# A fused attention and mixture-of-experts kernel: key stores and stack loads issued ahead of weight loads, and the first routing spread anew

## The chip, the cores and the metric
The kernel runs on one core of one Trainium2 chip. The metric is the device time of one launch in microseconds. TensorE (PE), VectorE (DVE), ScalarE (ACT) and GpSimd (POOL) compute, SyncE (SP) issues nearly all DMAs.

## The reference
Input x is 32 batches of 128 rows by 128; ctx has the same shape.

```python
x = x + tanh(g_xattn) * xattn(layernorm(x), ctx, ...)   # 16 heads of 8, keys of x and of ctx
#   q, k, v = layernorm(x) @ Wqkv + b ; qa, ka, va = ctx @ Wqkv_aux + b_aux
#   out = softmax(q k') v * (1 - gate) + softmax(q ka') va * gate ; out @ Wo + bo
x = x + tanh(g_ffn) * ffn(layernorm(x), ...)            # 64 experts of width 64, plus a shared one
#   scores = sigmoid(x @ gate_w.T); best 4 of 8 groups, best 8 experts in them, weights summed to 2.5
#   y = sum over experts e of cw[:, e] * (silu(x @ We_gate[e]) * (x @ We_up[e])) @ We_down[e]
```

## The kernel before
**Two phases.** First the attention over 32 blocks (one batch each), two blocks to a chunk, 16 chunks (NC = 16), four blocks to a body, 8 bodies (LOOPS = 8). Then the experts over 8 pieces of 512 rows, 33 pairs of experts each. The program is written out by hand: each engine has its own order of instructions, and semaphores tie them together.

**A chunk of the attention.** Queries and keys are split into three bf16 parts (`split`, on VectorE for chunks 0 and 1, on GpSimd from chunk 2 on; semaphore `lo_ok` counts its last steps, one for the queries and two for the keys). SyncE stores the parts to DRAM (`store_q` L411, `store_k` L418) and loads them back in another layout, heads one above the other, as `stack_q` (`load_stack_q` L431) and `stack_k` (`load_stack_k` L444). A load waits until its store has landed, and until TensorE has used the chunk three before in the same of three slots (`st_mm`). `clear_shift` (L436) copies zeros from `zero_d` into four rows of the slot. TensorE scores block b + 2 (`round_of_scores`, L1283), VectorE takes the maxima (L991), whose negatives go as rows into `stack_q` by a DMA that ScalarE issues (`shift_rows`, `stack_q<-nmaxT`). Then TensorE scores block b once more, shifted (L1307), ScalarE takes the exponentials (L791), TensorE weighs the values (`weighted`, L1322; it waits for the residual of the block before last), and VectorE adds the residual (L1034).

**SyncE's order in a chunk n** is that of `body` in `on_sp`: load x of n + 4, stack load of q of n + 2, clearing, two loads of expert weights (480 KB in most chunks), store of k of n + 2, stack load of k of n + 2, store of x2 of n - 1, store of q of n + 3. The expert weights are asked for by ScalarE (`high_of`) from chunk 2 on, two pairs a chunk.

**The first routing.** The last body (chunks 14 and 15, blocks k = 0 to 3 of `body` with `last`) also routes the first piece of the experts on VectorE: `first_route`, 14 parts, placed by `ROUTE_AT` at (block k, half-round u). In blocks 0 and 1 VectorE still takes maxima, in 2 and 3 not. TensorE turns the routing weights (`first_turn_w`), ScalarE copies them (`first_wT`, `fwt_ev`), SyncE stores them (L570) and loads them back, broadcast, as combine weights `cwb` (L578, two groups of two loads of 384 KB), which GpSimd's first products (`hidden`, L1631) wait for.

**The start.** SyncE stores zeros from `x2[0]` to `zero_d` (L513) ahead of the first q store.

Of the kernel before, what the change touches and what calls it, by code (L numbers as in the profile page):

```python
# [18 lines left out]
BF16 = mybir.dt.bfloat16  # L19
# [23 lines left out]
E, F = 64, 64  # L43
# [128 lines left out]
def attention(nc, sem, m, m_cw, psum, v):  # L172
    wide = v["wide"]
    x, ctx, x2d, q_d, k_d = v["x"], v["ctx"], v["x2d"], v["q_d"], v["k_d"]
    q0_d, k0_d, zero_d = v["q0_d"], v["k0_d"], v["zero_d"]
# [3 lines left out]
    NEX, NP, gwT, wts_d, cw_in, cwb, GP = (v[n] for n in ("NEX", "NP", "gwT", "wts_d", "cw_in", "cwb", "GP"))  # L179
# [11 lines left out]
    x2 = [m(f"x2_{i}", [P, CH, P], F32) for i in range(2)]  # L191
# [92 lines left out]
    def part(name, n):  # L284
# [33 lines left out]
    zeros_ok, zeros_st = sem("zeros_ready"), sem("zeros_stored")  # L318
# [32 lines left out]
                + [(n, c, r) for n in range(LIGHT, NC - 1) for c in range(CH) for r in (0, 3)]  # L351
                + [(NC - 1, 0, 1), (NC - 1, 0, 2), (NC - 1, 1, 0)])
    assert len(SPLIT_AT) == NP
    ROUTE_AT = {(0, 5): (0,), (0, 7): (1, 2), (1, 1): (3,), (1, 3): (4,), (1, 5): (5,), (1, 7): (6, 7), (2, 1): (8, 9),
                (2, 3): (10, 11), (2, 5): (12, 13)}

    STATS_AT = ((0, 5), (0, 7), (1, 1))

# [40 lines left out]
    def on_sp(sp):  # L399
# [7 lines left out]
        def store_q(n, i):  # L407

            wait(sp, lo_ok, SPLITS * n + 1)
            dst = q_d[n].rearrange("s p c t -> p s (c t)")  # L410
            sp.dma_start(dst[:, 0:PART], parts_q[i][:]).then_inc(q_st[i], 16)  # L411
            sp.dma_start(dst[:, PART], parts_q[i][:, Q_AT[0]]).then_inc(q_st[i], 16)

        def store_k(n, i):

            wait(sp, lo_ok, SPLITS * (n + 1))
            dst = k_d[n].rearrange("s p c a t -> p s (c a t)")
            sp.dma_start(dst[:, 2:2 + PART], parts_k[i][:]).then_inc(k_st[i], 16)  # L418
            sp.dma_start(dst[:, 0:2], parts_k[i][:, 0:2]).then_inc(k_st[i], 16)
# [14 lines left out]
        def clear_shift(n):  # L434

            sp.dma_start(stack_q[n % NST][64:68].rearrange("p h c t -> p (h c t)"), zero_d).then_inc(shift_zero[n % NST], 16)  # L436

        def load_stack_k(n):

            s = n % NST  # L440
            wait(sp, st_mm, UNITS * CH * (n - NST + 1))
            wait(sp, k_st[n % 2], 32 * ((n + 1) // 2))
            for half in (1, 0):
                sp.dma_start(stack_k[s][PARTS_AT[half]:PARTS_AT[half] + ROWS_S].rearrange("p h c a t -> p (h c a t)"),  # L444
                             pairs(k_v[n], 2 * DH, half, 2 * HH * TC)).then_inc(stk[half][s], 16)
# [53 lines left out]
        def store_x2(n, i):  # L499
# [9 lines left out]
        sp.dma_start(bo_row[:], one(v["bo"]).to_broadcast([P, P])).then_inc(wo_in, 16)  # L509
        load_x(2)  # L510
        load_x(3)
        sp.wait_ge(zeros_ok, 1)
        sp.dma_start(zero_d.rearrange("r (j t) -> (r j) t", j=4), x2[0][0:16].rearrange("p c t -> p (c t)").bitcast(BF16)  # L513
                     ).then_inc(zeros_st, 16)
        store_first_q()
        store_first_k(0)
        sp.wait_ge(stack_zero, 2)
# [6 lines left out]
        load_stack_q(1)  # L524
        load_stack_k(1)
        store_q(2, 0)

        def body(g, last):
            for j in range(2):
                n, i = 2 * g + j, j  # L530
                if n == 0:
                    sp.wait_ge(w_zero, 3)
                if n + 4 < NC:
                    load_x(n + 4)
                if not last:
                    if n == 0:
                        sp.wait_ge(stack_clear, NST)
                    load_stack_q(n + 2)
                    if n == 1:
                        sp.wait_ge(zeros_st, 16)  # L540
                    if n + 2 >= NST:
                        clear_shift(n + 2)
                if g < LOOPS - 2:
                    expert_weights(g, j)
                elif not last and j == 0:
                    expert_weights(g, 0)
                    expert_weights(g, 1)
                if not last:
                    store_k(n + 2, i)
                    load_stack_k(n + 2)  # L550
                if n > 0:
                    store_x2(n - 1, 1 - j)
                if n + 3 < NC:
                    store_q(n + 3, 1 - i)
                if g == 0:
                    small_weights(j)
                if g == LOOPS - 3 and j == 1:

                    for t in range(2):
                        sp.wait_ge(x2_st[t], 16)  # L560
                    sp.dma_start(xld[:], x2_four[0]).then_inc(xl_in, 16)
# [11 lines left out]
        for i in range(2):  # L573
            sp.wait_ge(q_st[i], 32 * (NC // 2 - 1 + i))
            sp.wait_ge(k_st[i], 32 * (NC // 2 - 1 + i))
        for gr in range(2):
            for half in range(2):
                sp.dma_start(cwb[gr][half * F:(half + 1) * F, :, :],  # L578
                             wts_v[0][half][GP * gr:GP * (gr + 1)].unsqueeze(0).to_broadcast([F, GP, T])
                             ).then_inc(cw_in[gr], 16)  # L580
# [145 lines left out]
    def on_act(act):  # L726
# [134 lines left out]
        def body(g, left):  # L861
            last, before_last = left == 0, left == 1
            for k in range(BODY):
                b, n, i, odd = BODY * g + k, 2 * g + k // CH, k // CH, k % CH
                first = b == 0
                more = not (last and i == 1)
                for r in range(ROUNDS):
                    exps(b, r)
                    if r == 0 and not first:
                        copy_o(b - 1, 1 - odd)  # L870
                    if r == 0 and not odd and n > 0 and n + 3 < NC:
                        norm(n + 3)
                    if (n, odd, r) in SPLIT_AT:
                        q = SPLIT_AT.index((n, odd, r))
                        if 2 * q + 1 < E - LAST_E:
                            act.wait_ge(w_in[0], 16 * 4 * (1 + max(0, -((FIRST_E - 2 * q - 2) // EACH_E))))
                        if q == NP - 1:
                            act.wait_ge(w_zero, 3)
                            act.wait_ge(w_in[1], 16 * 3)
                        if q == (E - LAST_E) // 2:  # L880
                            act.wait_ge(w_in[2], 16 * 4)
                        high_of(q)
                    if r == 1 and not (last and k == BODY - 1):
                        shift_rows(b + 1)
                    if before_last and k == 2 and r < 2:
                        if r == 0:
                            act.wait_ge(k_st[0], 32 * (NC // 2 - 1))
                        first_norm(r)
                    if before_last and k == 3 and r == 1:
                        first_operand()  # L890
                        act.wait_ge(lo_ok, SPLITS * NC)
                        first_xT()
                    if last and k == 0 and r == 0:
                        first_exp()
                    if first and r == 1:
                        norm(3)
                    if (odd, r) == ((0, 2) if last else (0, 1)) and more:
                        if first:
                            act.wait_ge(v_zero, 6)
                        copy_v(n + 1, (i + 1) % 2)  # L900
                    if odd and r == 1 and n + 3 < NC:
                        copy_qk(n + 3)
                    if r == 2 and not first:
                        copy_att(b - 1, 1 - odd)
                    if not odd and r == 2 and n + 3 < NC:
                        evac_t(n + 3, 1 - i)
                    if before_last and k == 2 and r == 3:
                        first_gate()
                    if last and k == 3 and r == 1:
                        first_wT()  # L910

        for g in range(LOOPS - 2):
# [8 lines left out]
    def on_dve(dve):  # L921
# [135 lines left out]
        def first_route(part):  # L1057
# [3 lines left out]
            sig, sp = f_sig_p, f_sc_p  # L1061
            halves = lambda t: t.rearrange("p k (g h e) -> p k g h e", g=NG, h=2)
            if part == 0:
                dve.wait_ge(fe_ok, 1)
                nc.vector.tensor_scalar(sig, f_sig[:].rearrange("p k e -> p (k e)"), 1.0, None, ALU.add).then_inc(fs_ok, 1)
                dve.wait_ge(fs_ok, 1)
                nc.vector.reciprocal(sig, sig).then_inc(fs_ok, 1)
            if part == 1:
                dve.wait_ge(fs_ok, 2)
                logit = sig.rearrange("p (k g h e) -> p k g h e", k=K, g=NG, h=2)  # L1070
                bias = gbias[:].unsqueeze(1).to_broadcast([P, K, E]).rearrange("p k (g h e) -> p k g h e", g=NG, h=2)
                for h, to in ((0, sp), (1, f_sc_s[:])):
                    tt(to.rearrange("p (k g) e -> p k g e", k=K), logit[:, :, :, h], bias[:, :, :, h],
                       ALU.add).then_inc(frt, 1)
# [161 lines left out]
    def on_pe(pe):  # L1236
# [171 lines left out]
        def body(g, left):  # L1408
            last, before_last = left == 0, left == 1
            for k in range(BODY):  # L1410
# [4 lines left out]
                for r in range(ROUNDS):  # L1415
# [41 lines left out]
                        first_turn_x()  # L1457
                    if before_last and k == 3 and r == 3:
                        first_logits()
                    if last and k == 3 and r == 0:  # L1460
                        first_turn_w()

        for g in range(LOOPS - 2):
# [558 lines left out]
```

## Time and profile before

| | us |
|---|---|
| median of 3 runs | 912.15 (909.82 to 915.29) |
| the profiled execution | 910.34 |
| its span | 908.5 |
| busy: TensorE, VectorE, GpSimd, ScalarE | 850.6, 677.4, 617.1, 563.5 |
| mean granted clock of TensorE | 0.983 |
| attention | 0 to about 329.6 |
| experts | about 329.6 to the end |

All times are counted from the start of the span. In a timeline row the first number is the start, the second the duration, and the bracket gives how long the engine was idle before and what ended that. SPq is SyncE's queue: a row there is the issue of a DMA, not its transfer.

### The profile page before, as it was taken

To read this page: it belongs to the slowest core of one execution; us is meant where nothing else is said; L and a number is where in the kernel's file an instruction comes from. 1 tells how busy PE (TensorE), PEld (TensorE's weight loads), DVE (VectorE), ACT (ScalarE), POOL (GpSimd) and SP (SyncE) were. 2 spreads that over 40 slices of the span, in tenths; PEclk is the share of its full clock that TensorE was granted. 3 is DMA by queue.
4 is the path that set the end of the run, shared out by engine and by line. 5 is a ranking of instruction groups with operands and counts; after the bars stand their busy time and mean duration, and the time that the engine had idled before them with its cause. 6 is when DMAs were issued, how large, how long until landed. Compare 5 with 4: busy or idle time off the path is not lost.

```text
span 908.5 us, 20053 instructions
## 1 busy us (share of the span) xinstructions
PE 850.6 (94%) x6765; PEld 647.7 (71%) x6765; DVE 677.4 (75%) x1653; ACT 563.5 (62%) x963; POOL 617.1 (68%) x579
## 2 busy tenths in 40 slices
PE   5789889899998889999999999999999999999997
PEld 3356556566665567888888888887888888888885
DVE  6788769686887857967866976977777776786665
ACT  4277668686777667557557556555656655755554
POOL 2455675576655337887877877787777777878785
PEclk9999999898999999999999999999999999999999
DMA  5666667666765044654654654754654655465552
GB/s 134 181 159 160 174 158 180 157 173 160 171 166 142 10 101 116 151 138 112 164 122 121 158 141 109 162 124 112 165 129 123 152 127 141 108 159 123 138 140 62
DMA packets 113755, 125.46 MB, mean 138 GB/s; under 512 B 28005, under 2 KB 76021, under 8 KB 112217
## 3 DMA queue, kind: packets, MB, share of 16 engines
q1 hardware_dynamic: 110776, 123.66, 55.6%
q10 hardware_dynamic: 2880, 0.59, 0.4%
q8 instruction: 49, 0.80, 0.4%
q14 instruction: 50, 0.40, 0.2%
HBM read 103.73 MB, written 19.97 MB: 136 GB/s over the span
## 4 chain that ended last, share of the span: by engine, by line
PE 70%; DMA 14%; POOL 4%; SPq 4%; DVE 3%; issue 3%; ACT 1%; POOLq 0%; ACTq 0%; DVEq 0%
PE bank L1928 18%; PE bank L1930 18%; PE bank L1929 18%; DMA stack_k<-k_scratch 6%; PE bank L1322 3%; DMA k_scratch<-parts_k 3%; PE bank L1307 2%; PE bank L1261 2%; DMA stack_q<-nmaxT 2%; PE bank L1283 2%; DMA q_scratch<-parts_q 1%; POOL hid L1631 1%; PE bank L1249 1%; SPq L431 1%; PE bank L1905 1%
## 5 line engine op out<-in xcount | busy, mean ns | idle before, releaser
L1631 POOL TENSOR_TENSOR hid<-act,cwb 128x512 f32<-128x512 f32 x264 | 430.7, 1639 | 134.3 <-DVE act L1846 92.2
L1680 ACT ACTIVATE silu<-bank 128x512 f32<-128x512 f32 x264 | 157.3, 596 | 209.6 <-PE bank L1930 209.5
L1846 DVE TENSOR_TENSOR act<-silu,bank 128x512 f32<-128x512 f32 x264 | 180.4, 684 | 142.8 <-ACT silu L1680 136.4
L1928 PE MATMUL bank<-xhi,weights_hi 128*128 128x512 f32 x528 | 210.0, 398 | 0.0
L1930 PE MATMUL bank<-xlo,weights_hi 128*128 128x512 f32 x528 | 207.8, 394 | 0.0
L1929 PE MATMUL bank<-xhi,weights_lo 128*128 128x512 f32 x528 | 207.3, 393 | 0.0
L1850 DVE TENSOR_TENSOR hlo<-hid,hhi 128x512 fp32r<-128x512 f32 x264 | 200.8, 761 | 2.7 <-ACT hhi L1685 2.5
L991 DVE TENSOR_REDUCE mx<-bank 128x4 f32<-128x512 f32 x256 | 164.7, 686 | 43.3 <-PE bank L1283 40.0
L1685 ACT ACTIVATE hhi<-hid 128x512 fp32r<-128x512 f32 x264 | 165.0, 625 | 8.0 <-POOL hid L1631 7.5
L791 ACT ACTIVATE prob<-bank 128x1024 f32<-128x1024 f32 x128 | 131.0, 1024 | 60.9 <-PE bank L1307 59.1
L1930 PEld LDWEIGHTS bank<-xlo,weights_hi 128*128 128x128 f32 x528 | 99.2, 188 | 22.3
L1928 PEld LDWEIGHTS bank<-xhi,weights_hi 128*128 128x128 f32 x528 | 99.3, 188 | 21.4 <-ACT silu L1680 0.3
L1929 PEld LDWEIGHTS bank<-xhi,weights_lo 128*128 128x128 f32 x528 | 99.4, 188 | 20.8
L1928 PE MATMUL bank<-hhi,weights_hi 128*128 128x512 f32 x264 | 104.4, 395 | 2.8 <-DVE hlo L1850 2.7
L1929 PE MATMUL bank<-hhi,weights_lo 128*128 128x512 f32 x264 | 103.6, 392 | 0.0
L1930 PE MATMUL bank<-hlo,weights_hi 128*128 128x512 f32 x264 | 103.3, 391 | 0.0
L1283 PE MATMUL bank<-stack_k,stack_q 48*128 48x256 bf16 (+1 forms) x512 | 60.3, 290 | 28.0 <-DMA stack_k<-k_scratch 21.6
L1322 PE MATMUL bank<-prob,V 128*32 128x128 f32 x2048 | 84.2, 283 | 0.0
L1322 PEld LDWEIGHTS bank<-prob,V 128*32 128x32 f32 x2048 | 48.9, 110 | 21.9 <-issue 15.5
L1928 PEld LDWEIGHTS bank<-hhi,weights_hi 128*128 128x128 f32 x264 | 49.6, 188 | 15.7 <-issue 2.4
L1930 PEld LDWEIGHTS bank<-hlo,weights_hi 128*128 128x128 f32 x264 | 49.7, 188 | 11.4
L1929 PEld LDWEIGHTS bank<-hhi,weights_lo 128*128 128x128 f32 x264 | 49.7, 188 | 11.2
(227 smaller groups left out, 939.9 us busy)
## 6 DMA issues: line engine op xcount, KB each, us to landing
cwb<-wts_scratch SPq DMA_DIRECT2D x176, 384.0 KB, 5.4
stack_k<-k_scratch SPq DMA_DIRECT2D x30, 384.0 KB
k_scratch<-parts_k SPq DMA_DIRECT2D x15, 384.0 KB, 4.5
stack_q<-q_scratch SPq DMA_DIRECT2D x30, 192.0 KB
k_scratch<-parts_k SPq DMA_DIRECT2D x15, 256.0 KB, 4.9
q_scratch<-parts_q SPq DMA_DIRECT2D x15, 192.0 KB, 3.0
xin<-in_x_dram SPq DMA_DIRECT2D x16, 128.0 KB, 2.8
cin<-in_ctx_dram SPq DMA_DIRECT2D x16, 128.0 KB, 3.3
```

The lines of the kernel that those rows point to most:

```text
L791: act.activation(prob[pair % RP][:].rearrange("p u k -> p (u k)"), wide[:], ACT.Exp, scale=scale).then_inc(p_ok, 1)
L991: nc.vector.tensor_reduce(mx[par][:, 2 * f:2 * f + 2, 2 * r:2 * r + 2].rearrange("p a h -> p h a"), s_bank[f].rearrange("p (h a k) -> p h ...
L1283: ins = nc.tensor.matmul(s_bank[f][:, e * TC:(e + 1) * TC], q_of(n)[at, 2 * r + e, c, :], k_of(n)[at, 2 * r + e, c].rearrange("p a t -> p ...
L1322: ins = nc.tensor.matmul(to, V[i][:, a, par, h, :], prob[(ROUNDS * b + u // 2) % RP][:, j % 2, (2 * a + j // 2) * P:(2 * a + j // 2 + 1) * P],
L1631: pool.tensor_tensor(h_buf[k][:], a_buf[k][:], cwb[slot][:, q % GP, :], ALU.mult).then_inc(h_ok, 1)
L1680: act.activation(s_buf[k % RS][:], g_bank[k % 2][:], ACT.Silu).then_inc(s_ok, 1)
L1685: act.activation(hhi[k % RH][:], h_buf[k % RS][:], ACT.Copy).then_inc(hh_ok, 1)
L1846: nc.vector.tensor_tensor(a_buf[k % RS][:], s_buf[k % RS][:], u_bank[k % 3][:], ALU.mult).then_inc(a_ok, 1)
L1850: nc.vector.tensor_tensor(hlo[k % RH][:], h_buf[k % RS][:], hhi[k % RH][:].bitcast(F32), ALU.subtract).then_inc(hl_ok, 1)
L1928: nc.tensor.matmul(bank, w[0], mh, start=first, stop=False)
L1929: nc.tensor.matmul(bank, w[1], mh, start=False, stop=False)
L1930: return nc.tensor.matmul(bank, w[0], ml, start=False, stop=last)
```

## The change
In each chunk SyncE issues the key store and the stack load of the keys ahead of the two weight loads. The store of zeros moves from ahead of the first q store to behind the stack loads of chunk 1 and the q store of chunk 2. The second group of the first combine weights is issued only when the first has landed. The reciprocal of the first sigmoids is cut in four steps of 64 columns, and the parts of the first routing get other places; their transposes on TensorE and the copy on ScalarE move one round later.

```diff
-    ROUTE_AT = {(0, 5): (0,), (0, 7): (1, 2), (1, 1): (3,), (1, 3): (4,), (1, 5): (5,), (1, 7): (6, 7), (2, 1): (8, 9),
-                (2, 3): (10, 11), (2, 5): (12, 13)}
+    ROUTE_AT = {(0, 3): (0,), (0, 5): (1 / 4,), (0, 7): (2 / 4,), (1, 3): (3 / 4,), (1, 5): (1,), (1, 7): (2,), (2, 1): (3, 4),
+                (2, 3): (5, 6, 7), (2, 5): (8, 9, 10), (2, 6): (11, 12, 13)}
...
         load_x(3)
-        sp.wait_ge(zeros_ok, 1)
-        sp.dma_start(zero_d.rearrange("r (j t) -> (r j) t", j=4), x2[0][0:16].rearrange("p c t -> p (c t)").bitcast(BF16)
-                     ).then_inc(zeros_st, 16)
         store_first_q()
...
         store_q(2, 0)
+        sp.wait_ge(zeros_ok, 1)
+        sp.dma_start(zero_d.rearrange("r (j t) -> (r j) t", j=4), x2[0][0:16].rearrange("p c t -> p (c t)").bitcast(BF16)
+                     ).then_inc(zeros_st, 16)
...
                         clear_shift(n + 2)
+                    store_k(n + 2, i)
+                    load_stack_k(n + 2)
                 if g < LOOPS - 2:
                     expert_weights(g, j)
                 elif not last and j == 0:
                     expert_weights(g, 0)
                     expert_weights(g, 1)
-                if not last:
-                    store_k(n + 2, i)
-                    load_stack_k(n + 2)
...
         for gr in range(2):
+            if gr == 1:
+                sp.wait_ge(cw_in[0], 32)
...
-                    if last and k == 3 and r == 1:
+                    if last and k == 3 and r == 2:
                         first_wT()
...
+            if 0 < part < 1:
                 dve.wait_ge(fs_ok, 1)
-                nc.vector.reciprocal(sig, sig).then_inc(fs_ok, 1)
+                cols = slice(int(4 * part - 1) * E, int(4 * part) * E)
+                nc.vector.reciprocal(sig[:, cols], sig[:, cols]).then_inc(fs_ok, 1)
             if part == 1:
-                dve.wait_ge(fs_ok, 2)
+                dve.wait_ge(fs_ok, 4)
+                nc.vector.reciprocal(sig[:, 3 * E:], sig[:, 3 * E:]).then_inc(fs_ok, 1)
+                dve.wait_ge(fs_ok, 5)
...
-                    if last and k == 3 and r == 0:
+                    if last and k == 3 and r == 1:
                         first_turn_w()
```

## Rows read from the trace of the kernel before
**Rows 1.** Windows: stretch, its length, busy time of each engine, clock, DMA share, GB/s.
```profile
58.84:296.50 237.66, 213.55 (x3427) 146.06 (x3427) 185.65 (x457) 172.70 (x274) 143.78 (x234) 0.95 0.67 165
132.90:136.30 3.40, 3.40 (x30) 2.54 (x23) 1.15 (x4) 1.85 (x4) 2.43 (x3) 0.51 0.42 110
296.50:329.60 33.10, 28.73 (x488) 18.07 (x487) 24.49 (x89) 24.06 (x36) 9.01 (x11) 0.95 0.09 23
345.00:908.50 563.50, 555.26 (x2474) 450.93 (x2473) 416.41 (x967) 333.06 (x595) 432.38 (x272) 1.00 0.54 131
```
**Rows 2.** Waits of TensorE, 58.5 to 296.5: us in total, times, longest.
```profile
PE bank L1283 <- DMA stack_k<-k_scratch: 20.9, 9, 4.0
```
**Rows 3.** Timeline of TensorE, 112 to 150 us, rows behind a wait.
```profile
112.19 0.40 PE L1307 MATMUL bank<-stack_q,stack_k 64*128 64x128 bf16 x8 [0.86 <-DMA stack_q<-nmaxT]
132.05 0.47 PE L1283 MATMUL bank<-stack_k,stack_q 48*128 48x256 bf16 x4 [3.97 <-DMA stack_k<-k_scratch]
149.40 0.40 PE L1307 MATMUL bank<-stack_q,stack_k 64*128 64x128 bf16 x8 [0.50 <-DMA stack_q<-nmaxT]
```
**Rows 4.** Timeline of SyncE's queue, parts of three chunks.
```profile
116.64 0.60 SPq L418 DMA_DIRECT2D k_scratch<-parts_k  x1
...
124.47 1.56 SPq L444 DMA_DIRECT2D stack_k<-k_scratch  x2
...
127.67 0.93 SPq L412 DMA_DIRECT2D q_scratch<-parts_q  x1
...
132.90 1.56 SPq L431 DMA_DIRECT2D stack_q<-q_scratch  x2
...
135.45 0.73 SPq L488 DMA_DIRECT2D weights_raw<-in_L_ffn_We_down_dram  x1
136.22 0.60 SPq L418 DMA_DIRECT2D k_scratch<-parts_k  x1
...
141.94 1.56 SPq L444 DMA_DIRECT2D stack_k<-k_scratch  x2
...
283.54 0.58 SPq L418 DMA_DIRECT2D k_scratch<-parts_k  x1
...
288.00 2.47 SPq L444 DMA_DIRECT2D stack_k<-k_scratch  x2
```
**Rows 5.** Timeline of GpSimd: last steps of a q split and a k split.
```profile
126.57 0.67 POOL L634 TENSOR_TENSOR parts_q<-rest,parts_q 128x256 bf16<-128x256 f32 x1
...
132.08 0.67 POOL L634 TENSOR_TENSOR parts_k<-rest,parts_k 128x256 bf16<-128x256 f32 x1
```
**Rows 6.** Chain of work that ended last: start, duration, two rows of maxima.
```profile
143.77 5.58 DMA stack_q<-nmaxT
...
216.60 6.79 DMA stack_q<-nmaxT
```
**Rows 7.** List of DMA issues: count, size, median us from issue to landing.
```profile
weights_raw<-in_L_ffn_We_gate_dram SPq DMA_DIRECT2D x5, 320.0 KB, 5.1
```
**Rows 8.** Timeline of VectorE at the start: last step of the first q split.
```profile
12.93 0.42 DVE L1166 TENSOR_TENSOR parts_q<-rest,parts_q 128x256 bf16<-128x256 f32 x1
```
**Rows 9.** Timeline of VectorE in the last body: parts of the first routing.
```profile
303.26 1.75 DVE L1067 RECIPROCAL f_sigmoid<-f_sigmoid 128x256 f32<-128x256 f32 x1
...
309.27 0.21 DVE L1083 TENSOR_TENSOR f_mid_b<-f_top_p,f_top_s 128x64 f32<-128x64 f32 x1
...
316.71 0.15 DVE L1108 MATCH_REPLACE8 f_grest<-f_gtop,f_gs 128x8 f32<-128x8 f32 x1
...
322.46 0.43 DVE L1149 TENSOR_TENSOR f_rep<-f_masked,f_wsum_p 128x256 f32<-128x256 f32 x1
```
**Rows 10.** Timeline of TensorE, 308 to 340 us, two rows behind a wait.
```profile
308.18 0.22 PE L1347 MATMUL bank<-ident_bf,nmax 128*128 128x128 bf16 x1 [1.01 <-DVE nmax L1003]
...
339.95 0.47 PE L1928 MATMUL bank<-hhi,weights_hi 128*128 128x512 f32 x1 [2.01 <-DVE hlo L1850]
```
**Rows 11.** Chain of work that ended last, at the start of the experts.
```profile
329.21 7.40 DMA cwb<-wts_scratch
```

## The prediction
> **What bounds the kernel now.** I read the windows first, to split the span into stages. From 345 us to the end (the experts) TensorE is busy 555.3 of 563.5 us at full clock [rows 1]; nothing of the change lies there, so that stage is taken as it is. The attention's steady part, 58.84 to 296.50, is another matter: TensorE is busy 213.6 of 237.7 us and its mean clock is 0.95 [rows 1]. Its list of waits says for whom: 20.9 us in nine waits are for stack_k [rows 2].
>
> TensorE's own timeline shows how a chunk (two batch rows, 13 of them in this stretch, so 18.28 us each) goes. It restarts at 112.19 and is back at the next chunk's scores at 132.05 - 3.97 = 128.08: 15.9 us of work. Then it waits 3.97 us for stack_k; the next chunk runs 132.05 to 148.90, 16.85 us, and waits 0.50 us for the row of maxima [rows 3]. That chunk took 1.0 us longer because the granted clock was half (0.51) from 132.9 to 136.3, right behind the wait [rows 1]. A mean clock of 0.95 is 237.7 x 0.05 / 0.5 = 24 us at half clock, seven such stretches; at 1.0 to 1.3 us each they cost some 8 us. So per chunk: 15.9 work, 1.85 waiting (24.1 / 13), 0.6 slow clock.
>
> SyncE's timeline shows why stack_k is late. Its slot comes free only when the chunk before has used it, so the load must fit into one chunk, behind the key store. One round [rows 4]: k store issued at 116.64, k load at 124.47 (7.8 us: SyncE stood on the store's landing), landed at 132.0, 7.5 us later. The q store, whose last part was ready at 127.24 [rows 5] and which was issued at once, landed only at 132.87, 0.9 us behind the k load; only then did the q load of the next chunk go out (132.90), then the weights (135.02 to 136.18), then the k store at 136.22, though GpSimd had the last k part at 132.75 [rows 5]; k load 141.94. So the stage turns in a loop: q landed, q load and row clearing 2.1 us, weights' issue 1.2, k store to k load 5.7 to 7.8, k load 7.3, q store behind it 0.9: 17.3 to 19.3 us, which spans the 18.28 seen.
>
> **Part 1: key store and stack load ahead of the weights.** Three things change.
> (a) Issue: the store leaves before the two weight issues, 1.2 us here, but never before GpSimd is ready. Over the chunks of this stretch SyncE's weight issues took 1.1 to 2.6 us and in two of them GpSimd was the later; I take 1.1.
> (b) The store no longer shares the DMA engines with 480 KB of weights. The one store that had none ahead of it went from 283.54 to 288.00, 4.46 us, against 5.72 (136.22 to 141.94) and 7.83 in the round above [rows 4]; I take 4.3 for 5.9, a gain of 1.5. Bounds: nothing, and 3.3.
> (c) The weights now stand behind the stack load, on the same queue, and ahead of the x2 store and of the q store of the next chunk. Everything on SyncE's queue behind them is later. The k load itself should keep its 7.3 us.
> Now the loop anew, from TensorE's restart T. GpSimd's q parts are ready at T + 15.05 and its k parts at T + 20.56 (127.24 and 132.75 less 112.19) [rows 3, 5]; they hang on VectorE's and TensorE's place in the chunk, not on the DMAs. Three bounds follow for the chunk length C.
> First, the k path, over two chunks: 20.56 + 0.3 + 4.3 + 7.3 = 32.4, so C = 16.2.
> Second, the q path: q landed to k store 2.1, k load 4.3, landed 7.3, weights X, q store 0.9: C = 14.6 + X. X has no row, as weights never stood there. Below: 0, if they fill gaps of the load (the DMA share was 0.67 [rows 1]). Above: 5.1 us, the whole median landing of a weight transfer [rows 7]. 480 KB at this stage's mean of 165 GB/s [rows 1] is 2.9; partly overlapped I take X = 2.1, C = 16.7.
> Third, the row of maxima: issued at T + 11.7 in the chunk with the slow clock, T + 10.4 without it, landed 5.58 to 6.79 us later beside a k load [rows 6]: C = 16.0 to 17.2. This is what is late next when stack_k is not.
> All lie above the work of 15.9. I take C = 16.7: waits of 0.8 us a chunk. After waits of 0.50 us no slow stretch is seen, after 3.97 one is [rows 1, 3], so the slow clock should mostly go with them. The gain is 13 x (18.28 - 16.7) = 20.5 us; with C = 15.9 it is 31, with 17.6 it is 9. The weights themselves come some 6 us later, landing near the start of the next chunk; ScalarE first asks for a chunk's weights half a chunk after that, so it stays covered; without that cover its exponentials would stand behind the wait.
> A rule speaks against this edit. The Trainium skill, DMA: Bandwidth & Descriptors, section "Queues, rings and completion order", says that each DMA engine takes the descriptors of one ring in ring order, and that SyncE has one ring per engine; by it the weights pass whole ahead of the q store. The trace agrees in one place: the q store, issued three microseconds into the k load, landed 0.9 us behind it. By that rule X is nearer to the weights' full time than to nothing, which is the rival below.
>
> **Part 2: zeros stored later.** The first q store waits for a part that VectorE had only at 12.93 + 0.42 = 13.35 [rows 8], and SyncE issued it 0.1 us later. So the zero store's own issue (0.5 us) was hidden behind that wait; 0.1 us at most is gained. At its new place it is followed by the wait of chunk 0, and its readers come 20 us later: nothing.
>
> **Part 3: sigmoids in four, route later.** In the last body (chunks 14 and 15) nothing is transferred and VectorE sets the pace: the stage 296.50 to 329.60 has TensorE busy 28.7 of 33.1 us and its clock is 0.95 [rows 1]. The reciprocal of 256 columns stands 1.75 us in front of the maxima [rows 9]; TensorE waited 1.01 us for VectorE at 308.18 [rows 10], and in this stretch 4.2 us in eight waits. Four steps of 1.75 / 4 = 0.44 us, one between two maxima, fit where VectorE has slack. Parts 3 to 7 of the route (23 instructions from 309.27 to 316.86, 2.6 us with their steps) [rows 9] move into the block where no maxima are left, so the routing weights are done 2.6 us later against that block's start: 322.9 becomes 325.5 in the old time, less what the two blocks before gain. The residual stands behind it on VectorE, and the last block's weighted sums wait for that; 0.5 us is lost there. Gained in blocks one and two: about 2.5 us of waits and 1.0 us of slow clock. Net 3.0, bounds 1 and 4.5.
>
> **Part 4: combine weights in two steps.** Their transposes and their copy move one round (1.6 us) nearer to the end of the attention. The store of 2.0 us and the loads follow: before, four loads shared the engines and the first pair landed at 336.61, 7.40 us after its second issue [rows 11]. Alone, that pair of 384 KB each should take what a stack load of the same size takes from its second issue, 6.7 us or a little less; I take 6.0, so 1.4 of the 1.6 comes back. TensorE waited 2.01 us for what hangs on it [rows 10]; I leave that. The second pair goes out 6 us later, needed three hidden products (4.2 us) and a root later: just in time, with TensorE two pairs ahead. SyncE's wait also holds the last x2 store and the third group's loads by some 1.5 us; both have that slack. Net 0, bounds -2 and +2.
> The fit of the Trainium skill (DMA: Bandwidth & Descriptors, section "Anatomy of one DMA"), a fixed 2.0 us and then 436 GB/s, would land that pair in 3.8 us; the sum would then be 2 us lower. No row here moves 768 KB that fast.
>
> **Sum.** 20.5 + 0.1 + 3.0 + 0 = 23.6 us. The profiled execution took 910.34 us for a span of 908.5, 1.8 less than the median of 912.15. 912.15 - 23.6 = 888.5; I say 889.
>
> **The rivals.**
> Everything vanishes (C = 15.9, X near 0, the row of maxima keeps pace): 31 + 3 + 2 = 36 us, 877. For it: the share of 0.67 leaves room. Against it: the row of maxima was late by itself in four chunks where stack_k was not, as at 149.40 [rows 3].
> The weights take the gap partly back: X = 3 to 3.5, C = 17.6 to 18.1, waits long enough that some of the slow stretches stay: 5 to 9 us here and 3 in the last body, 903 down to 900. For it: the order on the queue.
> Slower: the loop is closed by the weights. Where 14.6 + X passes 18.28, that is from X = 3.7 us on, this edit loses. With X = 5.1 a chunk is 19.7, 13 of them lose 18 us, less 3 from the last body: 927; just past the point, at X = 4.2, 912 + 7 - 3 = 916. Against it: in the old order the same weights lengthened the k store by only 1.5 us.
> It doesn't do what it says: if GpSimd's k parts were always the later, (a) is nothing, and (b) alone is left; that is in my range (C = 17.3).
>
> **Chances.** Forecast (C from 16.2 to 17.3, 880 to 897) 0.60; all vanishes (below 880) 0.11; partly taken back (897 to 907) 0.18; about no change 0.05; slower 0.06. The range 879 to 903 leaves out about 2 in 10. Within 0.5% (4.6 us, about what a measurement can tell from no change) are 907.6 to 916.7. Faster 0.88, same 0.06, slower 0.06.
>
> **What would show it.** Right: k store to k load 4 to 4.6 us; stack_k waits down from 20.9 to under 8 us in all; mean clock of the steady part 0.98 or more; waits for the row of maxima up; the q store landing 2 to 3 us after TensorE's restart. Wrong: a q load issued more than 3.5 us after the restart (X too small), a k load of over 8 us (weights interleaved), chunks still of 18 us, or TensorE's wait before the first down projection over 3 us.

## The result

The changed kernel takes 913.38 us (median of 20 runs) beside 909.87 us for the kernel before (20 runs); the ratio is 1.0037, 95% interval 1.002 to 1.0055. Where 889 us was forecast, it is 3.5 us slower. (The forecast took its 23.6 us off 912.15 us, a median of 3 runs; with 20 runs the kernel before is at 909.87.) The profiled execution has a span of 912.1 us and a mean clock of 0.963.

The attention's steady part, windows of the kernel after over 58.8 to 298.3 (its last chunk starts 1.5 us later than before), columns as in [rows 1], and TensorE's waits in it beside [rows 2]:

```profile
58.80:298.30 239.50, 216.85 (x3436) 148.28 (x3436) 185.90 (x457) 173.19 (x275) 144.54 (x236) 0.94 0.69 164
```
```profile
PE bank L1312 <- DMA stack_q<-nmaxT: 11.8, 8, 2.5
PE bank L1288 <- DMA stack_k<-k_scratch: 11.6, 6, 3.6
```

The chunk is as long as it was, 239.5 / 13 = 18.4 us. The wait for stack_k fell from 20.9 to 11.6 us, and the wait for the row of maxima took its place: 11.8 us in eight places, where the kernel before has 3.9 us in five. The clock is not better either: 0.94.

SyncE's queue in one round of the kernel after, which answers to [rows 4]:

```profile
134.59 1.56 SPq L431 DMA_DIRECT2D stack_q<-q_scratch  x2
...
137.05 0.38 SPq L418 DMA_DIRECT2D k_scratch<-parts_k  x1
...
142.62 1.56 SPq L444 DMA_DIRECT2D stack_k<-k_scratch  x2
144.23 0.59 SPq L485 DMA_DIRECT2D weights_raw<-in_L_ffn_We_up_dram  x1
...
147.92 0.39 SPq L411 DMA_DIRECT2D q_scratch<-parts_q  x1
148.35 1.21 SPq L412 DMA_DIRECT2D q_scratch<-parts_q  x1
...
153.98 1.56 SPq L431 DMA_DIRECT2D stack_q<-q_scratch  x2
...
164.80 2.75 SPq L411 DMA_DIRECT2D q_scratch<-parts_q  x1
```

TensorE at the two restarts around it, beside [rows 3], and the chain of work for one row of maxima, beside [rows 6]:

```profile
131.43 0.47 PE L1288 MATMUL bank<-stack_k,stack_q 48*128 48x256 bf16 x4 [1.93 <-DMA stack_k<-k_scratch]
149.86 0.47 PE L1288 MATMUL bank<-stack_k,stack_q 48*128 48x256 bf16 x4 [1.14 <-DMA stack_k<-k_scratch]
```
```profile
218.62 7.35 DMA stack_q<-nmaxT
```

The stack load goes out at 142.62 and has landed when TensorE restarts at 149.86; the q store, issued in full by 149.56 with the weights in front, lets the q load go only at 153.98, 4.1 us behind TensorE's restart, where before it was 0.9 us behind. Even its issue now takes 1.21 us, and 2.75 us a chunk later, where [rows 4] has 0.93.

The loop in three legs, each the mean over 12 chunks from SyncE's timeline (q load issue to k store issue; to the stack load's issue; to the next q load's issue). "Row" is the mean time from the issue of a row of maxima to TensorE's restart, over the rows that TensorE waited for (1 in e9, 5 to 11 in the other runs). These are the late rows of each run, not its average row:

| kernel | q load to k store | to k load | to next q load | sum | row |
|---|---|---|---|---|---|
| before | 3.8 | 6.0 | 8.7 | 18.5 | 5.9 |
| after | 2.4 | 4.6 | 11.5 | 18.5 | 6.6 |
| the order alone (e1) | 2.2 | 4.7 | 11.3 | 18.2 | 6.7 |
| no weights in these chunks (e4) | 2.7 | 4.4 | 9.2 | 16.3 | 6.0 |
| weights between (e6) | 2.8 | 4.6 | 9.7 | 17.1 | 5.8 |
| weights behind the q store (e7) | 2.3 | 5.1 | 9.7 | 17.2 | 5.9 |
| new order, whole rows (e8) | 2.4 | 4.6 | 10.8 | 17.8 | 6.7 |
| old order, whole rows (e9) | 3.5 | 5.3 | 8.9 | 17.7 | 6.0 |
| the change, weights between (f2) | 2.6 | 4.8 | 9.3 | 16.7 | 5.7 |

The first two legs gained 2.8 us and the third gave 2.8 back.

In the last body, TensorE and VectorE of the kernel after (beside [rows 9, 10]):

```profile
307.63 0.22 PE L1352 MATMUL bank<-ident_bf,nmax 128*128 128x128 bf16 x1 [0.26 <-DVE nmax L1004]
...
316.90 0.22 PE L1352 MATMUL bank<-ident_bf,nmax 128*128 128x128 bf16 x1 [1.66 <-DVE nmax L1004]
...
326.48 1.03 PE L1327 MATMUL bank<-prob,V 128*32 128x128 f32 x16 [1.83 <-issue]
...
342.92 0.47 PE L1933 MATMUL bank<-hhi,weights_hi 128*128 128x512 f32 x1 [2.19 <-DVE hlo L1855]
```
```profile
325.69 0.42 DVE L1154 TENSOR_TENSOR f_rep<-f_masked,f_wsum_p 128x256 f32<-128x256 f32 x1
326.04 0.34 DVE L1035 SCALAR_TENSOR_TENSOR x<-bank,tg_x,xin 128x128 f32<-128x128 f32 x1
```

The wait at the first row of maxima fell from 1.01 to 0.26 us, but a wait of 1.83 us is new; it ends at 326.48, when VectorE has done the residual (326.04 + 0.34). The profile calls it "issue": it names nothing that ended it. That it was the residual is shown by f3 below.

### The profile page after: what moved, and what is told of

The parts are those of the page before. It is cut to its first block, busy times and chain, and to the rows that moved or that the text cites. A ratio compares the mean times of both kernels' runs of the same rounds, so it can differ in the third digit from the quotient of the medians.

```text
span 912.1 us, 20056 instructions
## 1 busy us (share of the span) xinstructions
PE 852.4 (93%) x6765; PEld 649.2 (71%) x6765; DVE 681.1 (75%) x1656; ACT 563.3 (62%) x963; POOL 616.0 (68%) x579
## 4 chain that ended last, share of the span: by engine, by line
PE 73%; DMA 14%; DVE 3%; issue 3%; POOL 2%; SPq 2%; ACT 2%; ACTq 0%; POOLq 0%; DVEq 0%
PE bank L1933 18%; PE bank L1935 18%; PE bank L1934 18%; DMA stack_k<-k_scratch 5%; DMA stack_q<-nmaxT 5%; PE bank L1327 4%; PE bank L1312 3%; PE bank L1266 2%; PE bank L1288 2%; PE bank L1254 1%; PE bank L1334 1%; DMA cwb<-wts_scratch 1%; DMA k_scratch<-parts_k 1%; POOL hid L1636 1%; PE bank L1910 1%
## 5 line engine op out<-in xcount | busy, mean ns | idle before, releaser
L1288 PE MATMUL bank<-stack_k,stack_q 48*128 48x256 bf16 (+1 forms) x512 | 60.0, 289 | 17.7 <-DMA stack_k<-k_scratch 12.7
L1312 PE MATMUL bank<-stack_q,stack_k 64*128 64x128 bf16 (+1 forms) x1024 | 53.4, 226 | 13.4 <-DMA stack_q<-nmaxT 11.9
L1312 PEld LDWEIGHTS bank<-stack_q,stack_k 64*128 64x128 bf16 (+1 forms) x1024 | 30.3, 97 | 41.0 <-issue 19.7
```

The costliest lines, as they stand in the source:

```text
L1312: ins = nc.tensor.matmul(st_bank[f][:, (2 * a + e) * P:(2 * a + e + 1) * P], k_of(n)[at, at_half, c, a, :], q_of(n)[at, at_half, c, :], st ...
```

## The experiments

Theory A: the weights have to pass somewhere in the loop; behind the stack load they hold up the q store and the row of maxima, by as much as they had held up the key store. Rivals: the order does gain, and other parts of the change eat it; or something else, such as GpSimd's splits, holds the loop whatever the weights do.

### The parts alone

**e1_order**: the kernel before with the new order of SyncE only.

```diff
+                    store_k(n + 2, i)
+                    load_stack_k(n + 2)
                 if g < LOOPS - 2:
                     expert_weights(g, j)
...
-                if not last:
-                    store_k(n + 2, i)
-                    load_stack_k(n + 2)
```

> The new order of SyncE alone, on the kernel before. Theory A (the weights, now between the k load and the q store, close the loop again): the whole stays within 3 us of the kernel before, chunks of 18 to 18.6 us, k store to k load near 4.7 us, the q load issued 3 us or more after TensorE's restart. Rival (the order gains what was forecast and another part eats it): 12 to 20 us faster, chunks of 16.7 to 17.3 us.

Measured: ratio to the kernel before 1.0012 (0.999 to 1.0034). So the forecast's 20 us are not there in the order alone; that rival is out. Its chunks take 18.2 us, as theory A says. Its waits of TensorE, 58.2 to 294.3:

```profile
PE bank L1306 <- DMA stack_q<-nmaxT: 12.8, 8, 2.8
PE bank L1282 <- DMA stack_k<-k_scratch: 11.8, 5, 3.3
```

**e2_route**: the sigmoids in four, the new `ROUTE_AT`, the turn and the copy one round later, nothing else.

> Only the sigmoids in four and the new places of the route, with the turn and the copy one round later. Theory: VectorE frees its first two blocks (2 to 3 us fewer waits there), but TensorE waits 1.5 to 2 us in the last block for the residual that stands behind the route, and the weights' copy is later: in all 1 to 2 us slower. Rival, as forecast: 3 us faster.

Measured: 1.0013 (0.9992 to 1.0035), not told from no change. In the trace, from TensorE's wait in the second round of the last body to the first down projection it is 43.3 us (296.49 to 339.79), before 41.9 (298.03 to 339.95): 1.4 us longer, with the same wait of 1.83 us.

**e3_cw**: the combine weights in two steps, nothing else.

```diff
         for gr in range(2):
+            if gr == 1:
+                sp.wait_ge(cw_in[0], 32)
```

> Only the combine weights in two steps. The first pair lands 1.5 us earlier than in the kernel before (6.6 instead of 8.1 us from its first issue). Theory: TensorE's wait before the first down projection, 2.0 us, falls to 0.5 and the slow clock behind it goes: 1.5 to 3 us faster. Rival: the second pair or the third group, issued later, is now waited for: no gain.

Measured: 1.0012 (0.9989 to 1.0036). The wait before the first down projection did fall by 1.0 us:

```profile
342.97 0.47 PE L1930 MATMUL bank<-hhi,weights_hi 128*128 128x512 f32 x1 [1.02 <-DVE hlo L1852]
```

A microsecond is below what the runs can tell. No slow clock followed the wait in this trace (1.00 from 330 to 345, 0.89 before), but ScalarE's normalised x2 was then late for TensorE by 0.9 us at 347.18, so nothing more came of it.

### No weights in the steady chunks

**e4_after_allw**: the kernel after, with all expert weight loads issued in chunk 0.

```diff
-                if g < LOOPS - 2:
-                    expert_weights(g, j)
-                elif not last and j == 0:
-                    expert_weights(g, 0)
-                    expert_weights(g, 1)
+                if n == 0:
+                    for gg in range(LOOPS - 1):
+                        expert_weights(gg, 0)
+                        expert_weights(gg, 1)
```

> The changed kernel with every expert weight load issued in chunk 0, so that the later chunks have no weights on the queue at all. The first two chunks get longer by some 20 us; only the chunks from 4 on are read. Theory A: without weights the loop has 14.6 us of its own, chunks fall to 16.2 to 16.6 us (key path), little slow clock. Rival B (something else than the weights holds the loop, such as GpSimd's splits or the row of maxima): chunks stay at 17.5 us or more.

Measured in one execution (922.55 us, with the load of all weights ahead): TensorE restarts at 125.25 and at 273.00, nine chunks later, 16.4 us each. Its window and waits there:

```profile
125.30:273.00 147.70, 140.50 (x2377) 96.34 (x2378) 128.60 (x318) 119.87 (x189) 104.59 (x173) 1.00 0.58 158
```
```profile
PE bank L1311 <- DMA stack_q<-nmaxT: 3.9, 5, 1.5
PE bank L1287 <- DMA stack_k<-k_scratch: 3.5, 3, 1.5
```

The clock is full and 7.4 us of waits are left in nine chunks. So the weights' 480 KB cost 2 us a chunk, in the old place (18.3 us) as in the new (18.4). GpSimd's splits don't hold the loop at 18 us; that rival is out.

### Where they stand

**e6_between**: the kernel before, weights behind the key store and ahead of SyncE's wait for its landing.

```diff
+                    store_k(n + 2, i)
                 if g < LOOPS - 2:
                     expert_weights(g, j)
...
                 if not last:
-                    store_k(n + 2, i)
                     load_stack_k(n + 2)
```

> Kernel before, with the two weight loads of a chunk issued behind the key store and ahead of SyncE's wait for its landing, so that they fill the pause of the queue before the stack load. Theory A (the weights take DMA time wherever they stand in the loop q load, k store, k load, q store): the k load, behind them, lands later by what the k store gains; chunks of 17.5 to 18.3 us, at most 5 us faster in all. Rival (only the place matters, the pause is free): chunks near 16.8 us, 15 us or more faster.

Measured: 0.984 (0.9809 to 0.987), 894.61 us, 14.8 us faster. One round of its SyncE queue:

```profile
203.13 0.38 SPq L418 DMA_DIRECT2D k_scratch<-parts_k  x1
203.55 0.49 SPq L419 DMA_DIRECT2D k_scratch<-parts_k  x1
204.07 0.64 SPq L485 DMA_DIRECT2D weights_raw<-in_L_ffn_We_up_dram  x1
205.09 1.13 SPq L488 DMA_DIRECT2D weights_raw<-in_L_ffn_We_down_dram  x1
207.61 1.58 SPq L444 DMA_DIRECT2D stack_k<-k_scratch  x2
```

The weights are issued in the 4.5 us in which SyncE waits for the key store anyway, and the stack load goes out as soon as without them (4.6 us behind the key store's issue, 4.4 in e4). They don't move wholly in that pause: they land 4.9 to 5.8 us behind their issue (median), so part of them moves beside the stack load. From 165.99 to 263.98, six chunks, it is 16.3 us a chunk; the six chunks before took 17.8 (59.44 to 165.99), and the mean of the table is 17.1. So most of the weights' 2 us is gone, not all of it, and why the early chunks are slower is open. My theory A in its strict form (they cost the same wherever they stand in the loop) falls here; the place decides.

**e7_behind_q**: the kernel before, k store and k load first, the weights behind the q store.

```diff
-                if g < LOOPS - 2:
-                    expert_weights(g, j)
-                elif not last and j == 0:
-                    expert_weights(g, 0)
-                    expert_weights(g, 1)
-                if not last:
                     store_k(n + 2, i)
                     load_stack_k(n + 2)
...
                     store_q(n + 3, 1 - i)
+                if g < LOOPS - 2:
+                    expert_weights(g, j)
+                elif not last and j == 0:
+                    expert_weights(g, 0)
+                    expert_weights(g, 1)
```

> Kernel before, with k store and k load first and the weight loads behind the q store, last in the chunk. The q store lands soon behind the k load again (2 to 3 us after its issue), but the q load of the next chunk is behind the weights. Theory A: the q load lands later and the k store behind it is stretched, chunks of 17.3 to 18.3 us. Rival (what cost the gain was only the q store's place behind the weights): chunks of 16.8 us, 15 us or more faster.

Measured: 0.9897 (0.9854 to 0.9939), 897.90 us, 11.5 us faster, with chunks of 17.2 us. The third leg fell from 11.3 (e1) to 9.7 us and the row of maxima lands in 5.9; the second leg grew from 4.7 to 5.1, with the weights now issued just ahead of q load and key store. Between the two expectations, nearer to the rival; e6 was 3.3 us faster, but the two intervals overlap.

### Pieces or bytes

The gate and up weights are read in pieces of 256 bytes, the down weights in 512. **e8_flat_new** has the new order and **e9_flat_old** the old one, both with the same bytes read as whole rows of 2560 bytes; the experts then compute with permuted weights.

```diff
-                         up[e0:e0 + ne].rearrange("e d f -> d e f")).then_inc(done, 16)
+                         up[e0:e0 + ne].rearrange("e d f -> (e d f)").rearrange("(p e f) -> p e f", p=P, e=ne)
+                         ).then_inc(done, 16)
...
```

> The new order alone, with the same bytes of expert weights read as whole contiguous rows (2560 and 2560 bytes) instead of pieces of 256 and 512 bytes. The weights stand in a wrong order in SBUF, so the experts compute with permuted weights. If the small pieces are what makes the weights dear: chunks of 16.5 to 17.2 us, 12 to 20 us faster than the kernel before. If it is their bytes: chunks stay at 17.8 us or more, within 5 us.

> The same contiguous weights in SyncE's old order; the experts again compute with permuted weights. If the small pieces are dear: faster than the kernel before by 5 us or more, and slower than the new order with the same weights by some 5 us (there the order would pay). If it is bytes: as the kernel before.

Measured: 0.9939 (0.991 to 0.9968) and 0.9957 (0.9934 to 0.9981), with 95,962 packets in place of 113,755. The pieces are worth 4 to 6 us in either order, so neither expectation holds in full, and the order makes no difference that can be told. As a chunk is still 17.7 to 17.8 us and not 16.4, most of the weights' cost is not in the pieces. e8 shows which wait is then left, 58 to 297:

```profile
PE bank L1308 <- DMA stack_q<-nmaxT: 16.7, 11, 2.3
PE bank L1284 <- DMA stack_k<-k_scratch: 5.1, 2, 3.7
```

With the weights behind the stack load the rows that TensorE waited for still took 6.7 us to land, and they ended its wait in 11 places. In the old order (e9) it did so once, with 0.9 us.

### The whole change with the weights elsewhere, and the route mended

**f2_after_between**: the kernel after, with the weights where e6 has them.

> The whole change, with only the weights put between key store and k load instead of behind the k load. Theory (the place of the weights alone took the gain): 11 to 15 us faster than the kernel before, 14 to 18 faster than the changed kernel; the row of maxima lands in 5.8 us instead of 6.6, the q load goes out 3 us behind the q store instead of 4.7 to 5.4. Rival (the other parts of the change hold the time): under 8 us faster than before.

Measured: 0.9827 (0.9777 to 0.9877), 894.88 us: 16 us faster than the kernel before, and 18.5 less than the change's 913.38. Its chunks are 16.7 us, the rows of maxima that TensorE waited for land in 5.7, and its steady part has a clock of 0.99. The one thing moved is the weights, so in the change it was their place behind the stack load that took the gain. Even so, no run reaches the 23.6 us of the forecast.

**f3_residual_first**: e2 with parts 11 to 13 of the route behind the residual.

```diff
-                (2, 3): (5, 6, 7), (2, 5): (8, 9, 10), (2, 6): (11, 12, 13)}
+                (2, 3): (5, 6, 7), (2, 5): (8, 9, 10), (2, 7): (11, 12, 13)}
```

> The sigmoids and the route as in the change, alone on the kernel before, but parts 11 to 13 of the route behind the residual on VectorE, not ahead of it. Theory (TensorE's 1.83 us wait in the last block is for that residual): the wait goes, and 1.5 to 2.5 us with it against the run with the route alone, so 0 to 1 us faster than the kernel before. Rival (the wait is for the routing weights): it stays, or moves to the turn of the weights.

Measured: 0.9985 (0.9957 to 1.0014). The wait of 1.83 us is gone, so it was for the residual; the stretch from the second round to the first down projection is 42.4 us (296.10 to 338.46), 0.9 less than e2 and 0.4 more than before. Its last body had more slow clock in this trace (0.81 from 312 to 330, against 0.91 in e2 and 0.95 before), so what the later route costs by itself stays open. The runs can't tell either difference.

**f1_between_cw** (e6 with the combine weights in two steps) and **f4_between_cw_route** (f2 with f3's route):

> Weights between key store and k load (the earlier run with this order took 14.8 us off), and the combine weights in two steps. Theory: the two are in different stages and add: TensorE's wait before the first down projection falls by 1 us again, so 15 to 17 us faster than the kernel before. Rival: the combine weights in two steps are worth nothing or cost: 13 to 15 us.

> All together: weights between key store and k load, combine weights in two steps, route with the residual first, zeros later. If everything adds: 16 to 19 us faster than the kernel before and the fastest of all. Rival: the later route still costs, and this is slower than the weights between alone with the two steps.

Measured: 0.9812 (0.977 to 0.9853), 895.10 us, and 0.9807 (0.9757 to 0.9857), 894.62 us. Both, e6 and f2 lie within each other's intervals. All beat both kernels; which of the four is best isn't told. In f1 the wait before the first down projection is 0.77 us (1.93 in e6). In f4 TensorE then waits 0.63 us for the routing weights themselves, at 304.74.

## Why the prediction was wrong

**What was right.** The reading of the loop, and its first two legs: the k store leaves earlier (3.8 to 2.4 us, against 1.1 forecast gain) and lands sooner (6.0 to 4.6, forecast 5.9 to 4.3). Without weights I gave 14.6 us to the q path and 16.2 to the k path; e4 has 16.4.

**Part 1 (c), the q path: the step that failed.** C = 2.1 + 4.3 + 7.3 + X + 0.9 with X = 2.1 was 16.7. e1 measures 2.2, then 4.7, then 11.3 for the rest; the sign that the prediction names for too small an X came too (in the kernel after the q load goes out 4.1 us behind the restart, over 3.5). In the chunks where TensorE waited for stack_k, the load landed 7.8 us behind its issue (7.4 before), which leaves 3.5 for X + 0.9; with the 0.9 kept, X = 2.6. The terms were 0.1 (q load), 0.4 (key store), 0.5 (stack load) and 0.5 (X) too small, all with the same sign: together 1.5 us a chunk, 20 us in 13. That "the k load itself should keep its 7.3 us" was wrong, and X was taken near its lower half on the ground of a DMA share of 0.67, a mean over the chunk. What counts is probably the share behind the stack load, where the x2 store, the q store and the x loads stand too; what that row of transfers shows is that its members land later (in e1; before: 2.9 us for the q store, 5.1 for the weights):

```profile
q_scratch<-parts_q SPq DMA_DIRECT2D x12, 192.0 KB, 4.4
weights_raw<-in_L_ffn_We_gate_dram SPq DMA_DIRECT2D x5, 320.0 KB, 7.6
```

So the 5.1 us from [rows 7], my upper bound for X, was itself a time of the old place. The rule that spoke against the edit pointed the right way, though X stayed below the 3 to 3.5 us of its rival. The Trainium skill (DMA: Bandwidth & Descriptors, section "Queues, rings and completion order") has each engine take one ring's descriptors in order; the trace agrees in direction: e7, which only moves the weights behind the q store, gave 1.6 us of the third leg back.

**Part 1, the row of maxima.** I had its bound as C = 16.0 to 17.2 and took it to stay. For the rows that TensorE waited for it rose with the edit: 5.9 us to land before, 6.7 in e1 and e8, 5.8 to 5.9 in e6 and e7. The row is 16 KB on ScalarE's queue, and I had asked for every wait behind the weights on SyncE's queue only. 10.4 + 6.7 = 17.1, and with a slow clock ahead of it 11.7 + 6.7 = 18.4. How the 18.2 us of e1 divide between the q path and the row I can't say: in e1 the row ended the wait in eight places and stack_k in five; with whole rows (e8) the third leg is 10.8 us and the row ends 11 of 13 waits, 16.7 of 21.8 us, at 17.8 us a round. No run relieves the row and keeps the q path as it is, so how much each is worth stays open.

**The clock.** I counted 8 us of slow clock as mostly gone, on waits of 0.8 us. The waits stayed at 1.8 a chunk and the clock with them (0.94). In e4 and in the six good chunks of e6 it is 1.00. The term was conditional on the others and had no value of its own.

**The weights' cost.** "In the old order the same weights lengthened the k store by only 1.5 us" was my ground against the slower rival. True, but they also cost 1.2 us of issue there, and 2.7 in all is about what came back in the third leg (2.6, from 8.7 to 11.3). The break-even X of 3.7 was set against 18.28 with the other terms as forecast; with 2.2, 4.7, 7.8 and 0.9 it is 2.7, and the real X was at it.

**Part 3.** Forecast 3.0 us gained, bounds 1 and 4.5; the trace has 1.4 lost. That is e2's trace; its runs can't tell it from nothing. Fewer waits in the first block came true (0.56, 0.31 and 0.75 us), but the second block's wait grew from 1.12 to 1.65, as part 2 stands on VectorE right in front of the steps that TensorE waited for, and the wait for the residual, named at 0.5 us, was 1.83. The step that failed here is the place of parts 11 to 13: I reckoned when the routing weights are ready, and not when TensorE would ask for the residual behind them.

**Part 4.** Forecast 0; e3 has a wait 1.0 us shorter, in the change the later copy took it back (2.19 against 2.01). The first pair landed at 339.59, 5.94 us behind its second issue (forecast 6.0, and 6.38 in e3); the 3.8 us that the prediction has from the Trainium skill (DMA: Bandwidth & Descriptors, section "Anatomy of one DMA") was not reached, and that fit is given for DMAs issued by GpSimd, not by SyncE. Here is the row, beside [rows 11]:

```profile
333.65 5.94 DMA cwb<-wts_scratch
```

**Part 2**, forecast at 0.1 us, was not measured by itself; TensorE's restart of the first steady chunk is at 58.77 after and 58.84 before.

**The range.** 903 as its upper end rested on X up to 3.5 with everything else kept. The terms were not independent: in e1 q store, stack load and row all grew at once behind one crowd, and they should have been moved together. Two small slips changed nothing: the loop's terms add up to 17.2 us at the least, not 17.3, and 912.15 - 36 is 876, not 877.

## What to carry to other kernels

Bulk transfers that nobody waits for belong into a pause in which the issuing queue waits for a landing, here between a store and the load that reads it back; there 480 KB cost 0.4 to 1.1 us a chunk (16.7 us in f2 and f4, 17.1 in e6, 17.4 in f1, against 16.3 without them), and ahead of the key store or behind the stack load 2. Last in the chunk, behind the q store, they cost 0.9 (e7), which isn't told from the pause. Before moving a transfer out of a critical leg, ask which leg it then stands in front of, and mind the small transfers of other queues too. In a sum over a loop, terms that hang on the same crowd err in the same direction: price them together.

## What the hardware showed that I had not expected

The issue of a DMA on SyncE is not a fixed 0.4 to 0.6 us. Behind the stack load, the weights and the x2 store it took 1.2 to 2.75 us (the latter at 164.80 in the kernel after). In the steady part, single issues above 1 us sum to 34 us in e1, 19 in the kernel after and 10 in the kernel before. But they sum to 22 us in f2 too, which is 16 us faster, so these figures alone don't say what they cost the loop.

A row of 16 KB on ScalarE's queue took 5.3 to 6.3 us where TensorE waited for it in e6 and f2. In e1 it took 6.1 to 7.9, with 480 KB of small pieces behind the stack load on SyncE's queue, though it is on another queue.
